# The order of ScalarE's work in an attention and a mixture-of-experts stage: copies for TensorE first, a sum copied sooner, a tail spread over more units

## The reference, cut to what matters

```python
mod = (_silu(L0_c) @ L0_wmod).reshape(L0_c.shape[0], 6, 1, -1)
sa, ca, ga, sb, cb, gb = (mod[:, 0], ..., mod[:, 5])
h = _layernorm(x) * (1 + ca) + sa
x = x + ga * attn(h)        # top 2 of 8 experts, causal linear attention in each, 8 heads of 16
h = _layernorm(x) * (1 + cb) + sb
x = x + gb * ffn(h)

def ffn(x):
    h = x @ lin0_w + lin0_b
    h = silu(h @ swi1_w1 + b1) * (h @ swi1_w2 + b2)
    h = moe(h)              # softmax router, top 4 of 8 experts, and a shared expert of double width
    h = h @ lin1_w + lin1_b
    return silu(h @ swi2_w1 + b1) * (h @ swi2_w2 + b2)
```

## Time and profile before

| | |
|---|---|
| median of three runs | 1312.92 us (1306.09 to 1319.36) |
| the profiled execution | 1298.82 us, its span 1297.1 us |
| busy in the span | TensorE 1090.8 us, VectorE 934.8, ScalarE 668.4, GpSimd 491.8 |
| mean granted clock of TensorE | 0.941 |

### The profile page before, as it was taken

How to read it: one execution, slowest core, us unless ns; L and a number is a source line. 1 busy time by engine, 2 the same in 40 slices (tenths; PEclk the granted TensorE clock), 3 DMA queues, 4 the chain that set the end, 5 groups by cost and what they waited for, 6 DMA issues and landing times. The chain is left out here.

```text
span 1297.1 us, 26776 instructions
## 1 busy us (share of the span) xinstructions
PE 1090.8 (84%) x9288; PEld 787.8 (61%) x9288; DVE 934.8 (72%) x2058; ACT 668.4 (52%) x1645; POOL 491.8 (38%) x450
## 2 busy tenths in 40 slices
PE   4875589999999887899988977778886799889996
PEld 3554456676676555566656645556664566667774
DVE  4774568788876665777778748787778887776664
ACT  2542245555555545556666535645555555445553
POOL 2057023313323544322211226656655433455542
PEclk8986689999999999999999989889888899999999
DMA  9962123323333333222222134123322023233220
GB/s 310 372 255 89 45 83 99 111 76 104 111 104 91 101 93 89 77 66 64 63 62 57 49 108 123 31 69 92 88 87 86 19 85 90 66 95 98 74 81 17
DMA packets 83586, 125.76 MB, mean 97 GB/s; under 512 B 9088, under 2 KB 65920, under 8 KB 79360
## 3 DMA queue, kind: packets, MB, share of 16 engines
q1 hardware_dynamic: 73216, 98.86, 25.0%
q0 software_dynamic: 10240, 25.18, 6.2%
HBM read 71.32 MB, written 52.69 MB: 96 GB/s over the span
## 5 line engine op out<-in xcount | busy, mean ns | idle before, releaser
L1486 DVE SCALAR_TENSOR_TENSOR att<-reach,endrel,wide 128x1024 f32<-128x1024 f32 x160 | 204.8, 1280 | 87.1 <-PE wide L1398 68.8
L1595 POOL TENSOR_TENSOR kvw<-kvw,hq 128x512 f32<-128x512 f32 x128 | 170.4, 1333 | 227.0 <-ACT kvw L1686 220.9
L898 POOL DMA_INDIRECT gst<-attended_rows,idxs x128 | 139.0, 1086 | 254.0 <-DVE att L1486 129.1
L1717 DVE TENSOR_TENSOR epp<-kvw,epp 128x512 fp32r<-128x512 f32 x160 | 153.8, 961 | 104.2 <-ACT epp L1691 102.1
L252 POOL DMA_INDIRECT routed_rows<-hq,idxs x128 | 132.0, 1031 | 224.6 <-DVE att L1486 150.3
L1640 PE MATMUL bank<-epp,w2p 128*128 128x512 f32 x480 | 172.2, 469 | 9.6 <-DVE epp L1717 9.4
L1686 ACT ACTIVATE kvw<-bank 128x512 f32<-128x512 f32 x160 | 94.5, 591 | 111.0 <-PE wide L1630 110.8
L1630 PE MATMUL bank<-hp,w1p 128*128 128x512 f32 x480 | 144.2, 410 | 5.7 <-POOL hp L1549 4.7
L1691 ACT ACTIVATE epp<-kvw 128x512 fp32r<-128x512 f32 x160 | 100.4, 628 | 92.3 <-DVE kvw L1724 92.1
L1373 PE MATMUL bank<-kvw,turned 128*128 x320 | 142.9, 529 | 5.5 <-ACT turned L1283 1.6
L1630 PE MATMUL wide<-hp,w3p 128*128 128x512 f32 x480 | 142.2, 406 | 0.0
(11 more groups left out here) (265 smaller groups left out, 1914.3 us busy)
## 6 DMA issues: line engine op xcount, KB each, us to landing
hq<-weight_rows SPq DMA_DIRECT2D x16, 2048.0 KB
routed_rows<-zero SPq DMA_DIRECT2D x4, 5120.0 KB, 24.5
rows<-routed_rows SPq DMA_DIRECT2D x80, 256.0 KB
attended_rows<-ob SPq DMA_DIRECT2D x80, 128.0 KB
out<-fin SPq DMA_DIRECT2D x16, 256.0 KB
routed_rows<-hq,idxs POOLq DMA_INDIRECT x128
gst<-attended_rows,idxs POOLq DMA_INDIRECT x128
hq<-in_ew SPq DMA_DIRECT2D x3, 512.0 KB, 6.7
```

The lines of the kernel that those rows point to most:

```text
L898: pool.indirect_dma_start(gst[:, u, k, :], None, orow[s], bass.IndirectOffsetOnAxis(idxs[:, t, k % TOPA:k % TOPA + 1], 0), bounds_check=BL ...
L1486: dve.scalar_tensor_tensor(out=att[:, n % 2, :, :], in0=reach[:, :, :].rearrange("p a c -> p (a c)").unsqueeze(1) .to_broadcast([P, 4, 2 * ...
L1595: pool.tensor_tensor(g, g, rows_of(b % 2, n, n + 1), ALU.mult).then_inc(s_eu, 1)
L1717: dve.tensor_tensor(epp[:, (k - 1) % RING, 1, :], ep[:, (k - 1) % RING, :], epp[:, (k - 1) % RING, 0, :], ALU.subtract).then_inc(s_el, 1)
```

## The change

In the attention stage ScalarE's order becomes: `keep_outputs`, `mask_k`, `keep_products`, `keep_turned`, `split_heads`, `output_rows`, then the job copies that a TensorE job waits for (`post_copies`, new: jt, jm, jh, js, the router's weights), then the other jobs (`post_act`, which keeps weightings, square, normalised rows and exponential).

In the expert stage ScalarE's order becomes: the gate of unit k, the tail, `post_copies`, the high part of k−1, `post_act`. The tail's units: the sum is copied at n=2 (was 3), T2 stays 3, ScalarE's Silu stays 4, T3 is 5 (was 4), VectorE's product 6 (was 5), the scaling 7 (was 5), T4 is 8 (was 6), the residual sum 9 (was 7). GpSimd makes the high part of the next batch's input at n=5 and the low part at n=6, with a semaphore between them where a drain was.

```diff
-        def hidden_parts(pool, b, u):
+        def parts_of(b):
+            u = b % 2
+            high, low = (hp[:, u, k, :].rearrange("p (i d) -> p i d", d=D) for k in range(2))
+            return h_all[:, b * NT:(b + 1) * NT, :], high, low
+
+        def high_part(pool, b):
+            h, high, low = parts_of(b)
             pool.wait_ge(s_h2, b + 1)
-            h = h_all[:, b * NT:(b + 1) * NT, :]
-            high, low = (hp[:, u, k, :].rearrange("p (i d) -> p i d", d=D) for k in range(2))
-            pool.tensor_copy(high, h)
-            pool.drain()
+            pool.tensor_copy(high, h).then_inc(s_hh, 1)
+
+        def low_part(pool, b):
+            h, high, low = parts_of(b)
+            pool.wait_ge(s_hh, b + 1)
             pool.tensor_tensor(low, h, high, ALU.subtract).then_inc(s_hl, 1)
...
-        SUM, T2, T3, T4 = 3, 3, 4, 6
+        SUM, T2, T3, T4 = 2, 3, 5, 8
...
-                    if n == 3 and 0 < b < NB - 1:
+                    if n == 5 and 0 < b < NB - 1:
                         pool.wait_ge(s_eg, NU * b)
-                        hidden_parts(pool, b + 1, (b + 1) % 2)
+                        high_part(pool, b + 1)
+                    if n == 6 and 0 < b < NB - 1:
+                        low_part(pool, b + 1)
...
-                    if n == T2 + 1:
+                    elif n == T2 + 1:
                         act.wait_ge(s_t2, b + 1)
...
-                    elif n == T3 + 1:
+                    elif n == T3 + 2:
                         act.wait_ge(s_t3c, b + 1)
...
                 for k in range(UNITS + NU):
                     b, n = divmod(k, NU)
-                    if b:
-                        tail(b - 1, n)
                     if b < NB:
                         act.wait_ge(s_eg, k + 1)
                         act.activation(eg[:, k % RING, :], gate_bank[k % 2][:, :], ACT.Silu).then_inc(s_es, 1)
+                    if b:
+                        tail(b - 1, n)
+                    post_copies(act, NBK + k)
                     if 1 <= k <= UNITS:
                         act.wait_ge(s_ep, k)
```

and in the attention stage:

```diff
                     if odd and here(h):
                         keep_outputs(h)
+                    if is_block(n + 4):
+                        mask_k(n + 4)
                     if is_block(n + 5):
                         keep_products(n + 5)
                     if not odd and here(h + 3):
                         keep_turned(h + 3)
-                    post_act(act, n)
+                    if odd and here(h + 2):
+                        split_heads(h + 2)
                     if odd and here(h):
                         output_rows(h)
-                    if odd and here(h + 2):
-                        split_heads(h + 2)
-                    if is_block(n + 4):
-                        mask_k(n + 4)
+                    post_copies(act, n)
+                    post_act(act, n)
```

More of the change, by code:

```diff
@@ L900, in post_pool, with post_copies @@
                                             bounds_check=BLOCKS[s] * P - 1, oob_is_err=False).then_inc(s_g[u], 16)
+        def post_copies(act, slot):
+            b = at(0, slot)
+            if b is not None:
+                act.wait_ge(s_onT, b + 1)
+                act.activation(jt[:, :], bank[3][:, :], ACT.Copy).then_inc(s_onc, 1)
+            b = at(1, slot)
+            if b is not None:
+                act.wait_ge(s_y, b + 1)
+                act.activation(jm[:, :], bank[3][:, :], ACT.Copy, scale=mods[:, 2, b:b + 1]).then_inc(s_yc, 1)
+            b = at(9, slot)
+            if b is not None:
+                act.wait_ge(s_fT, b + 1)
+                act.activation(jh[:, :], bank[3][:, :], ACT.Identity, bias=mods[:, 3, b:b + 1],
+                               scale=mods[:, 4, b:b + 1]).then_inc(s_fh, 1)
+            b = at(13, slot)
+            if b is not None:
+                act.wait_ge(s_w1, b + 1)
+                act.activation(js[:, :], bank[3][:, :], ACT.Silu, bias=bias[:, 1:2]).then_inc(s_sg, 1)
+            r = group(12, slot)
+            if r is not None:
+                act.wait_ge(s_wt, r + 1)
+                if r:
+                    act.wait_ge(s_cw, 16 * r)
+                act.activation(wrow[:, :, :], bank[3][0:E * NT, :].rearrange("q (b t) -> q b t", t=P),
+                               ACT.Copy).then_inc(s_wc, 1)
         def post_act(act, slot):
@@ L915, in post_act @@
                 act.activation(halves_of(b)[:, :, 1, :], halves_of(b)[:, :, 0, :], ACT.Square).then_inc(s_gq, 1)
[L916 to L923, removed]
             b = at(8, slot)
@@ L932, in post_act @@
                 ins.then_inc(s_fx, 1)
[L933 to L941, removed]
             r = group(2, slot)
@@ L945, in post_act @@
                 act.activation(ex[:, :, :], ex[:, :, :], ACT.Exp).then_inc(s_x1, 1)
[L946 to L952, removed]
         def post_pe(pe, slot):
@@ L1540, in adaln_block @@
         hp = tb("hp", [P, 2, 2, S], F32R)
+        s_hh = sem("hidden_high_part")
         s_hl = sem("hidden_parts")
-        def hidden_parts(pool, b, u):
+        def parts_of(b):
[4 more added lines that the diff above has]
+            h, high, low = parts_of(b)
             pool.wait_ge(s_h2, b + 1)
-            h = h_all[:, b * NT:(b + 1) * NT, :]
-            high, low = (hp[:, u, k, :].rearrange("p (i d) -> p i d", d=D) for k in range(2))
-            pool.tensor_copy(high, h)
-            pool.drain()
+            pool.tensor_copy(high, h).then_inc(s_hh, 1)
+        def low_part(pool, b):
+            h, high, low = parts_of(b)
+            pool.wait_ge(s_hh, b + 1)
             pool.tensor_tensor(low, h, high, ALU.subtract).then_inc(s_hl, 1)
@@ L1586, in _ @@
                 for b in range(2):
-                    hidden_parts(pool, b, b)
+                    high_part(pool, b)
+                    low_part(pool, b)
                 for k in range(UNITS):
```

## The result

The changed kernel took 1267.54 us in the median of four runs (1264.95 to 1272.62), the one before 1309.51 (four runs, 1305.64 to 1319.36): a ratio of 0.9673, 95% interval 0.9625 to 0.972, or 42 us less. The prediction was 1264 (1240 to 1290). The profiled execution took 1272.62 us, span 1270.8. It is the highest of its four, while the profiled one of before (1298.82) lies under all four of its own, so the two traces are only 26 us apart. The stage ahead of the change hides another 6 us: there the first score mask starts at 177.7 us instead of 171.8. I therefore compare stretch by stretch.

What follows compares the result with a forecast made beforehand. The bound was taken to be TensorE's waits on ScalarE's order, not its load, in expert batches with jobs. Expert stage 24 − 7 + 9 + 4 + 4 + 7 = 41, attention 8: 1312.92 − 49 = 1264 us, range 1240 to 1290.

Steps and rivals of the forecast that it cites:

- The hole and its cause: Expert batches with jobs: ScalarE's order makes TensorE's turn job wait for the modulated copy; 24.2 us go.
- GpSimd's parts: Expert stage: parts at n=5 and n=6 shorten TensorE's waits for the router's weights; 4 us gained, bounds 0 and 8.
- the waits for L948: Expert batches with jobs: longer waits for the normalised rows take back 1 us in each of seven batches, 7.
- The clock: Expert batches with jobs: with the holes gone the mean grant rises from 0.90; 9 us gained, bounds 0 and 20.
- Copies ahead of the high part: Expert stage: the high part comes about 1.1 us later, covered by the distance of three units; price 0.
- Rival 1: Expert stage: VectorE becomes the bound, low parts held under GpSimd instructions; 37 us less, 1276; chance 0.15.
- Sum a unit sooner: Late expert batches: TensorE's first tail product no longer waits for the sum; five by 0.75, 4 us.
- Batches 7 to 10: Expert stage: half of the 13.8 us without TensorE work goes, 7 us.
- Attention: Attention blocks with jobs: mask_k first ends the states' waits for it; 8 us less, bounds −11 and 15.
- 2: Expert stage: copies starve the down products, 1.1 us showing on TensorE each time; 30 us slower, 1343; chance 0.05.
- 3: Expert stage: holes move to the waits for the normalised rows, clock stays; 32 us less, 1281; chance 0.15.
- 4: Attention stage: mask_k delays the K copy by 0.42 us in half of 160 blocks; 14 less, 1299; chance 0.07.

Runs made afterwards that it cites:

- b4: The kernel before with only the gate moved ahead of the tail, whose steps keep their old units; ratio to the kernel before 0.9994.
- a2: The kernel before with the gate ahead of the tail and the tail spread, sum still copied at n=3; ratio to the kernel before 0.9893.
- a4: The changed kernel with the job copies put back behind the high part in the expert stage; ratio to the kernel before 0.964.
- a3: The changed kernel with GpSimd's high and low part back together at n=3, with the drain; ratio to the kernel before 0.9699.
- b1: The changed kernel with the sum copied at n=3 again; ratio to the kernel before 0.9748.
- a1: The kernel before with ScalarE's new order in the attention stage alone, expert stage unchanged; ratio to the kernel before 0.9823.
- d1: The kernel before with mask_k moved first in ScalarE's attention iteration and nothing else; ratio to the kernel before 0.9899.
- c0: The changed kernel, unaltered, timed again in the second session; 1263.66 us, ratio to the kernel before 0.9664.

## Why the prediction was right, point by point

*The hole and its cause.* Right: 24.2 us of waits for the modulated copy are gone, in the order of steps that was forecast. Which edit brings what was not forecast so: of the 21 us of batches 1 to 6 the gate ahead brings 3 by itself and loses them in the late batches (b4), gate and spread together 13 (a2). Taken back alone, the copies' new place is worth 6 (a4), GpSimd's parts 3 (a3) and the sum's move 1 (b1). The prediction had the copies at 0 and GpSimd's parts at 4. b4, a2 and b1 also show that the sum's move is no extra of 4 us but what makes the early gate affordable.

*Size in batches 1 to 6.* Forecast 24 − 7 + 9 + 4 = 30 with batch 7; measured 21.2 and nothing in batch 7 (32.7 and 32.9 us). 18 us of it are idle time of TensorE, 3 its busy time. The idle time by term, batches 1 to 6: the copy's 24.2 gone; the waits for L948 took back 3.1 us (8.1 to 11.2), about half of the forecast; the wait for the router's weights returned 3.0 (11.3 to 8.3) of the 4 forecast. Two terms were missing: the wait for L1026 grew by 3.1 us (3.5 to 6.6), and 3.0 us came in front of L966. The clock rose as forecast, 0.90 to 0.94, but gave 3 us of TensorE's busy time, not 9: 186.36 to 183.25. I took the missing grant for lost time; part of it fell on waits, where it costs nothing (in the wait from 906.2 to 910.4 of the earlier trace rows the grant was 0.81 with no matmul running).

*Copies ahead of the high part, at 0.* The cover held (4.9 us of waits for the low part in the repeated run), but the step was mis-sized in the other direction: it gains. Rival 1 named the right mechanism, a low part held up by a GpSimd instruction, with the wrong sign, though the note against it had it right: a low part 1.1 us later meets only the multiply's last tenths. Low parts got shorter, 961 to 825 ns.

*Sum a unit sooner.* Late batches 1.1 us each instead of 0.75, five of them 5.5 us for 4.

*Batches 7 to 10.* This term failed: forecast 7 of the 13.8 us without TensorE work, measured 1.4 of them (12.4 left), and TensorE's busy time rose by 2.6 (108.11 to 110.67) at a lower clock (0.93 against 0.97), so the stretch came out 1 us longer. The waits for the sum (1.9) and for the low parts (3.5) did go. In their place came 3.4 us for the router's weights in batch 10 and, in batch 9, 3.6 us for the tail's scaling instead of 1.7, from VectorE's router steps under GpSimd's parts. The clock's part may be no effect of the change: a1, with the old expert stage, has 110.85 us at 0.95 there.

*Attention.* Forecast 8; measured 10 in the two profiled executions, and from block 70 on, over the kernels with the old and new order, 6 to 12, in the first session 17. Cause right (the mask), and d1 shows that in its session it is nearly all of it.

*Rivals.* 2 needs a distance of two units. 3 did not come: L948 holds 2.8 us at most. 4 is excluded by d1.

*The sum.* 49 were forecast, 42 measured (interval 37 to 49) and 43 by c0. The terms agree less well than the total: by stretches the two traces show 21.2 − 1.2 + 5.5 = 25.5 us in the expert stage against 41, and 10 in attention against 8, 35.5 in all. The other 6 us of the medians are located nowhere; attention and the stage ahead of it vary by as much with no edit. So the cause and the direction were foreseen, but that the total fell into the range of 1250 to 1275 us, with an expert stage over-forecast by 15 us, is in part luck.

## What to carry to other kernels

When a step that waits is moved off a unit's path, move each step behind it as well: here the early gate alone brought nothing (0.9994), because the tail steps that fed TensorE in the same unit were now one gate late. Before an instruction is put in front of another at no cost, ask also what the later start makes it run beside; a delay can be a gain. Here low parts went from 957 to 825 ns because they began when GpSimd's multiply was nearly over. In a schedule with three busy engines, price the clock by TensorE's busy time in a stretch, not by its mean grant.

## What the runs showed of the hardware

The kernel before took 1240.36 us in the first session and 1306.92 and 1311.85 in the others. The first two sessions ran on the same chip, so a change of chip does not explain their difference. The expert stage has no part in it: its batches 1 to 6 took 232.8 us in a1, of the first session, and 233.8 in d1, of the third. The attention stage has: with the same order it took 538.6 us in a2 and 588.8 in b4, and 35 of these 50 us lie from block 70 on, where the jobs and their gathers run (325.1 and 360.2). The stage ahead of it has 17 (162.1 and 179.5). ScalarE's copy of the attended output (L1318) shows it. In the profiled execution of before it waited 15 times, 31.6 us in all, for an event to which the trace gives no source, behind `attend` matmuls whose records had ended up to 3.0 us earlier; in b4 14 times, 28.9 us, and in a2 never. In the stretch from 505 to 760:

```profile
ACT oTs L1318 <- PE bank L1443: 20.5, 17, 3.1
ACT oTs L1318 <- remote: 15.2, 8, 3.1
```

From block 86 on one such wait returns every ten blocks, at the same block of each batch. What holds TensorE there, and why it does so in two sessions and not in the first, stays open: no run of this study separates it.
